# Weights of the GNN's products in a PSUM bank, written by an exponent of their own

## The reference

```python
xn = layernorm(x)                                        # x: 6250 nodes x 256
x = x + gnn(xn, src, dst, W, att) + linear_attention(xn)
x = x + mixture_of_experts(layernorm(x))                 # routed by a second graph attention

def gnn(h, src, dst, W, att):                            # 100000 edges, 4 heads of 64
    z = einsum('ni,hoi->hno', h, W)
    e = leaky_relu(e_src[:, src] + e_dst[:, dst])
    ex = exp(e - segment_max(e, dst)[dst])               # softmax over the edges into a node
    alpha = ex / segment_sum(ex, dst)[dst]
    return segment_sum(alpha * z[src], dst)
```

## Time and profile before

| | |
|---|---|
| median of 3 runs | 2942.56 us (2938.81 to 2943.4) |
| the profiled execution | 2940.0 us |
| its span, first to last instruction | 2937.9 us |
| busy: VectorE, GpSimd, TensorE, ScalarE | 2121.8, 2013.1, 1496.6, 1206.4 us |
| the loop's gathers, first start to last end | 423.3 to 1401.2 us |

### The profile page before, as it was taken

How to read it: one execution, slowest core, us unless ns; L and a number is a source line. 1 busy time by engine, 2 the same in 40 slices (tenths; PEclk the granted TensorE clock), 3 DMA queues, 4 the chain that set the end, 5 groups by cost and what they waited for, 6 DMA issues and landing times. The chain is left out here.

```text
span 2937.9 us, 21979 instructions
## 1 busy us (share of the span) xinstructions
PE 1496.6 (51%) x5476; PEld 949.3 (32%) x5476; DVE 2121.8 (72%) x3413; ACT 1206.4 (41%) x2381; POOL 2013.1 (69%) x1978
## 2 busy tenths in 40 slices
PE   2657730222212222222125179999899999984323
PEld 1433330111111111111025046555555555551122
DVE  6978889998888888888568255565655555657657
ACT  1532338776667776666334022222222232221012
POOL 0456457777777777777666677777777777777560
PEclk8878875555555555555555589999999999997666
DMA  4522547666666666666563312222222222222186
GB/s 137 186 68 68 148 126 238 229 225 214 209 204 216 219 218 207 218 218 213 190 176 105 107 30 49 49 67 51 49 49 49 49 53 53 61 50 44 17 304 230
DMA packets 222462, 395.96 MB, mean 135 GB/s; under 512 B 50867, under 2 KB 174370, under 8 KB 214912
## 3 DMA queue, kind: packets, MB, share of 16 engines
q1 hardware_dynamic: 137604, 263.49, 26.2%
q0 software_dynamic: 75632, 122.58, 18.0%
q10 hardware_dynamic: 9100, 8.50, 0.9%
HBM read 204.85 MB, written 189.59 MB: 134 GB/s over the span
## 5 line engine op out<-in xcount | busy, mean ns | idle before, releaser
L1234 POOL DMA_INDIRECT stage_got<-ffn_rows,setup_src_ffn x860 | 844.2, 982 | 261.8 <-issue 261.7
L1234 POOL DMA_INDIRECT edges_got<-gnn_rows,edges_src_gnn x728 | 756.4, 1039 | 241.7 <-issue 221.5
L1341 DVE TENSOR_TENSOR_SCAN stage_y<-stage_decays,stage_y 128x960 f32<-128x960 f32 (+2 forms) x256 | 520.7, 2088 | 5.1 <-issue 5.0
L2174 PE MATMUL stage_ph<-ffn_xt_all,stage_w 128*128 128x448 f32 x896 | 381.5, 566 | 102.0 <-ACT stage_hid L2235 40.3
L1357 ACT ACTIVATE stage_rows<-stage_y 128x3640 f32<-128x3640 f32 (+1 forms) x88 | 399.8, 4543 | 0.0
L1630 PE MATMUL stage_pm<-setup_ident,stage_mix_parts 128*128 128x128 f32 x98 | 33.4, 444 | 674.6 <-DVE stage_mix_parts L1703 602.3
L2296 DVE TENSOR_TENSOR stage_start_parts<-stage_pk,stage_of_tile 128x490 f32<-128x490 f32 x328 | 209.2, 667 | 115.8 <-PE stage_pk L2166 111.1
L2166 PE MATMUL stage_pk<-stage_start_parts 128*128 128x490 bf16 x984 | 244.3, 386 | 66.9 <-DVE stage_start_parts L2296 51.9
L1317 DVE TENSOR_TENSOR stage_y<-edges_got,stage_y 128x896 f32<-128x896 f32 x168 | 262.9, 1672 | 0.3 <-ACT stage_y L1299 0.3
L2174 PEld LDWEIGHTS stage_ph<-ffn_xt_all,stage_w 128*128 128x128 f32 x896 | 173.8, 197 | 243.9 <-issue 141.9
L1630 PEld LDWEIGHTS stage_pm<-setup_ident,stage_mix_parts 128*128 128x128 f32 x98 | 14.2, 204 | 705.0 <-DVE stage_mix_parts L1703 677.3
(11 more groups left out here) (481 smaller groups left out, 2903.3 us busy)
## 6 DMA issues: line engine op xcount, KB each, us to landing
state_gnn<-stage_rows SPq DMA_DIRECT2D x56, 1848.0 KB
y<-search_found SPq DMA_DIRECT2D x28, 896.0 KB, 4.2
tail_fin_y<-y SPq DMA_DIRECT2D x7, 3584.0 KB, 17.7
stage_got<-ffn_rows,setup_src_ffn POOLq DMA_INDIRECT x860
edges_got<-gnn_rows,edges_src_gnn POOLq DMA_INDIRECT x784, 3.6
state_ffn<-stage_rows SPq DMA_DIRECT2D x32, 384.0 KB, 2.4
mix_rows<-stage_mix_parts SPq DMA_DIRECT2D x49, 131.0 KB, 2.1
x_again_mix<-mix_rows SPq DMA_DIRECT2D x7, 917.0 KB, 6.1
```

The source lines that it names most:

```text
L1234: pool.indirect_dma_start(out=got[:, u, t, :], out_offset=None, in_=self.row_dram[g.name][:, :], in_offset=bass.IndirectOffsetOnAxis(ap=sr ...
L1341: ins = dve.tensor_tensor_scan(some, r[s][:, 0:b - a, :].rearrange("p c t -> p (c t)"), some, 0.0, ALU.mult, ALU.add)
L2174: mm = pe.matmul(ph[:, f % 2 * 2 + half, 0:HALF], w1[:, e, k, f * P:(f + 1) * P], xt_all[:, k, at(b * (B * P) + half * HALF, HALF)], start ...
```

## The change

In the GNN's loop the edge weights are written twice. A new PSUM tensor `weights` of one bank takes exp(`pm`) first, and carries the semaphore `w_ready`; the exponent into y's last columns follows without a semaphore of its own, and the exponents into `decays` after it. VectorE's product reads its weights from the new tensor; ScalarE's share of the products still reads y. Nothing else is changed, and the FFN's code is as before.

```diff
         if g is GNN:
             decays = self.ps(stack, "decays", [P, 2, 1024])
+            weights = self.ps(stack, "weights", [P, 512])[:, 0:2 * H * T].rearrange("p (s h t) -> p s h t", s=2, h=H)
...
-                act.activation(y[:, s, C:C + H, 1:T + 1], pm[:, :, :], ACT.Exp).then_inc(w_ready, 1)
+                if g is GNN:
+                    act.activation(weights[:, s, :, :], pm[:, :, :], ACT.Exp).then_inc(w_ready, 1)
+                    act.activation(y[:, s, C:C + H, 1:T + 1], pm[:, :, :], ACT.Exp)
+                else:
+                    act.activation(y[:, s, C:C + H, 1:T + 1], pm[:, :, :], ACT.Exp).then_inc(w_ready, 1)
...
                     ins = dve.tensor_tensor(of_head(h, s)[:, :, :, 0:n].rearrange("p q k t -> p t q k"),
                                             mine.rearrange("p t (q k) -> p t q k", q=Q),
-                                            w[:, h, 0:n].unsqueeze(2).unsqueeze(3).to_broadcast([P, n, Q, KQ]), ALU.mult)
+                                            weights[:, s, h, 0:n].unsqueeze(2).unsqueeze(3).to_broadcast([P, n, Q, KQ]), ALU.mult)
```

## The result

| | before | after |
|---|---|---|
| median of 6 runs | 2940.18 us | 2870.77 us (2869.45 to 2873.43) |
| ratio, 95% interval | | 0.9766 (0.9754 to 0.9779) |
| the profiled execution, its span | 2940.0, 2937.9 | 2869.45, 2867.4 |
| mean of the 728 gathers | 1039 ns | 947 ns |

The kernel is 69.4 us faster by the medians, 70.5 by the profiled executions. The forecast was 2877, its range 2868 to 2894. In the new kernel L1235 is the gather (L1234 before), L1322 the product (L1317), L1346 the scan (L1341), L1251 the chunk's first logits step (L1250).

What follows compares the result with a forecast made beforehand. It took GpSimd's pace of gathers to bound the loop. 65 us off the gathers, with nothing for the other steps, took the profiled 2940.0 to 2875.0, on the runs' scale 2877 us; range 2868 to 2894.

Steps and rivals of the forecast that it cites:

- Step 1: GNN loop: with the product's weights in PSUM, gathers under it come down to 0.945 us, saving 65 us.
- rows 8: FFN scan with decays in SBUF: a gather starting 1.00 us into it takes 1.29 us, waiting for its end.
- Step 2: VectorE's product in the GNN loop: slow through its output's stride, so its duration stays 1.67 us.
- the fast end: VectorE's product at the unbroken rate, 1.09 us instead of 1.67: 3.5 us more gain, 2874 us, chance 0.2.
- Step 3: ScalarE, GNN loop: one more exponent per chunk, 0.2 us each, hidden by idle time, cost 0; uncovered, 11 us.
- Step 4: The stretch behind the gathers, from last landing to next stage, moves as a whole, its length unchanged.
- Rivals A to D: Gathers stay long (2942 us, 0.04); DMA eats gain (2905, 0.05); PSUM slows product (2887, 0.06); VectorE becomes bound (3110, 0.02).
- B: Gathers' landings: the DMA, beside stored rows, takes a third to a half of the gain, 2905 us, chance 0.05.

Runs made afterwards that it cites:

- x6: The changed kernel with one more product per chunk on VectorE, weights from PSUM, into a spare tensor nobody reads: 2914.49 us.
- x8: The changed kernel with five gather buffers instead of four, five gathers of chunk 4 issued in the stage before the loop: 2860.19 us.
- x1: The changed kernel with the new weights tensor in SBUF instead of PSUM: 2944.32 us, ratio 1.0 to the kernel before.
- x5: The changed kernel with the scans' decays in SBUF instead of PSUM, the products' weights still in PSUM: 3088.56 us.
- x7: The changed kernel with the three products writing in unbroken runs into a spare tensor nobody reads: 2879.91 us in a single run.
- x2: The changed kernel with products reading y as before, the exponent into PSUM made but unread: 2947.15 us, ratio 1.0009 to the kernel before.
- x3: The changed kernel with the last of three products (head 2) reading its weights from y in SBUF: 2913.04 us.
- x4: The changed kernel with the middle of three products (head 1) reading its weights from y in SBUF: 2928.88 us.

## Why the prediction was right

The bound was read rightly. The window's busy times alone name VectorE (852 against 756 of 978 us); the gaps of 0.30 us that nothing releases, added to GpSimd's busy time, give the whole window, and the waits for landings say the same. x6, where VectorE gets 1.56 us more and the sides change, and x8, where only GpSimd's start is moved and the end follows, confirm it. The sum for the profiled execution was 2875.0 and it took 2869.45. The 5.5 us are 2.4 of the gathers, 0.7 of the last landing, 0.4 between the last store and the next stage and 2.0 behind the loop.

**Step 1, the gathers under the product: right, a little too small.** I took 65 of the 68.4 us above the clean duration; the gathers gave back 67.2. Of the 68.4 us before, 65.8 were those of the 162 gathers that started under the product, so the 65 were nearly exact; the rest was that of the short instructions with two SBUF inputs, for which I had left 3 us. In the new kernel all 728 gathers together are 689.2 - 728 x 0.945 = 1.2 us above clean. The short instructions still hold what starts in them, but it starts later in them: under L1703 (L1708 after) 1.9 us over 17 gathers became 0.7 over 14. x1 shows that the place of the weights is the cause, x5 that it is the number of SBUF inputs and not the kind of instruction or the output. The sentence of the Trainium skill that I weighed against the rows ("SBUF — State Buffer", section "Who interferes with whom": tensor_tensor was not seen to stall descriptor generation, with a reason marked there as inferred) does not hold for these gathers: they took 1039 ns in the mean with two SBUF inputs and 947 with one. The general rule of that section, two SBUF inputs contend and one doesn't, is what the earlier trace rows, x1 and x5 show.

The trace before held a cleaner comparison than the scan of rows 8, which I had overlooked. L1703 and L1693 are VectorE instructions of one shape and one output pattern, the first with two SBUF inputs, the second with one in PSUM:

```profile
1385.76 0.40 DVE L1703 TENSOR_TENSOR stage_mix_parts<-stage_mix_parts 128x256 f32<-128x256 f32 x1
1385.83 1.15 POOL L1234 DMA_INDIRECT edges_got<-gnn_rows,edges_src_gnn  x1 [0.30 <-issue]
...
1293.30 0.42 DVE L1693 TENSOR_TENSOR stage_mix_parts<-stage_pq,stage_mix_parts 128x256 f32<-128x256 f32 x1
1293.42 0.95 POOL L1234 DMA_INDIRECT edges_got<-gnn_rows,edges_src_gnn  x1 [0.30 <-issue]
```

Six gathers started with 0.29 to 0.33 us of L1703 left and took 1109 to 1148 ns; twelve started with 0.29 to 0.34 us of L1693 left and took 942 to 947. Under the reduction L1697, which has a single input and that in SBUF, six that started with 0.31 to 0.35 us left took 946 to 951 ns. So it is the second SBUF input that holds, and a gather passes without any PSUM input too.

**Step 2, the product's duration: right.** It was left at 1.67 us because of the stride, and is 1.667; x7 shows the stride as the cause and 1.074 without it, where I had 1.09. What I had for the fast end was too much: of the 3.5 us x7 shows none at the start and 1.3 at the end. The forecast didn't use that term, but the lower end of the range did.

**Step 3, the exponent: near enough.** It takes 0.16 us from start to start, where I had 0.2. What it costs the total, which I put at 0, is 2.7 us in x2 with an interval that takes in zero.

**Step 4, what comes after: right.** Last gather, last chunk, last store and next stage moved by 67.4, 68.1, 68.1 and 68.5 us. The last chunk's wait behind its last gather shrank as well, from 2.6 to 1.9 us, which I hadn't counted.

The signs that I had named came out: last gather at 1333.8 (named: 1336), VectorE's waits of 1.1 us from the 23rd chunk on, mean gather 947 (about 950). Rivals A to D did not occur. B, the DMA taking part of the gain, is excluded by the landings: from a gather's start to its landing the median is 3.3 us after, 3.5 before.

## What to carry to other kernels

When GpSimd issues indirect DMAs in a row, look at their durations beside VectorE's instructions: a gather that is longer than the shortest one and started inside a VectorE instruction with two SBUF inputs is waiting for that one. If GpSimd's busy time and issue gaps fill the stage, put one input of the long instructions into PSUM; where only some can be moved, count which gathers start in the rest, since the first part of a long instruction costs most. Before speeding up the engine with the highest busy share, add up the other engines' gaps that nothing releases: x7 made VectorE's products 36% shorter, and GpSimd's pace stayed the same (a mean gather of 948 ns, 947 in the changed kernel).

## What the runs showed of the hardware

The hold is decided at the gather's start. In x3 and x4 together 110 gathers started while the product that reads SBUF ran; 108 were held and took its rest plus 0.70 to 0.73 us, whatever the rest was (0.45 to 1.64 us). The other two had started 6 and 9 ns behind the product's start; in x5 three that started 4 to 20 ns into a scan went free as well. Of the 67 that had started before the product or with it and reached into it none was lengthened (954 ns at most). A part of one shared instruction can therefore cost more than a share: one held product of three took back 40 to 54 of 69 us. VectorE hardly changed: the product's mean was 1672 ns with gathers held and 1667 with none, the scan's 2141 (x5) and 2139. What in the chip a held gather waits for, and why it then needs 0.70 to 0.77 us more, no run here shows. And a product of 896 elements written with a stride of 60 bytes takes 1667 ns, in unbroken runs 1074.
